# All inputs first, four convolutions in one go, and two expert sums moved to GpSimd, in a kernel of conditional convolution and quantized FFN

## Chip, cores and metric

One core of a Trainium2 chip. The metric is the device time of one execution in microseconds (us), lower is better; the median of repeated runs is compared. Engines: TensorE (PE), VectorE (DVE), ScalarE (ACT), GpSimd (POOL), SyncE (SP). PEld are TensorE's weight loads.

## What is computed

The reference, cut to its core. `x` has 32 tiles of 128 x 2048, `cond` is 32 x 128, there are K = 8 experts of 128 x 128, H = 2048 and I = 1024:

```python
h = gelu(gelu(cond @ W0 + b0) @ W1 + b1)
att = softmax(h @ W2 + b2)                                   # 32 x 8
agg_w = einsum('bk,koi->boi', att, weight)                   # one 128 x 128 matrix per tile
y = einsum('boi,bih->boh', agg_w, x) + (att @ bias_k)[:, :, None]
y = y.astype(bf16)
qg, sg = quant(y * inv_gate); qu, su = quant(y * inv_up)     # per row: max|.|/127, round, clip
gate = (qg @ w_gate.T) * sg * s_wgate
up   = (qu @ w_up.T) * su * s_wup
inter = clip(silu(gate) * up, -10, 10).astype(bf16)
qi, si = quant(inter * inv_inter)
out = x + (qi @ w_down.T) * si * s_wdown
```

## The kernel before

Each of the 32 tiles of x is one unit of work, `t`. For each tile the kernel mixes the eight expert matrices into one (`aggw`), convolves (`conv`, four fp32 matmul calls of 512 columns, each two instructions), writes y as bf16 (`conv_out` on ScalarE), multiplies y by `inv_gate` and reduces each row to its largest value (VectorE: `xg_product`, `xg_scale`, together `quant_g`), forms the codes (ScalarE's `quant_g`), transposes them (on TensorE for the first tiles, by `turn_g`, with an eviction `turned_g` on ScalarE; by a transposing DMA later), and multiplies them with `w_gate` (`gate`, 16 values of `k`, two matmuls each). The up branch is the same with `quant_u`, `turn_u`, `turned_u`, `up`. Then come silu, product, clip, the third quantization and `down`.

Every engine has its instruction order written out by hand, and semaphores join them. Tiles 0 to 3 (`EARLY` = 3, `FIRST` = 4) are handled in a prologue while the weights arrive; from tile 4 on the loop is regular. The change is to the prologue, but for one wait in GpSimd's loop.

Where the expert matrices of the first tiles are mixed:

- tile 0: VectorE sums five experts (`aggregate_first`), TensorE three (`aggregate_mm(0)`), by matmuls with diagonal matrices that ScalarE writes;
- tile 1: ScalarE scales the experts, VectorE reduces them (`experts_sum`, L1082);
- tile 2: GpSimd writes eight diagonal matrices (L465), TensorE sums (`aggregate_mm(2)`, 16 instructions at L538), ScalarE evicts (`aggregate_out`);
- tile 3: the same with VectorE's `diagonals(3)` (L1088);
- from tile 4 on: GpSimd's `aggregate`, four instructions (L442, L444, L446, L450).

`biases_first` (L1041, L1043, L1046) has to be through before `conv_out(0)`. `quant_first` takes tile 0's gate quantization in four chunks of 512 columns (product L1165, reduction L1172). The codes' reciprocal scales are written at L1103; ScalarE's quantization waits for them.

SP's queue loads, in this order: the small MLP inputs, the experts, x0, `inv_gate`, x1, the row vectors, x2, and, once w_gate's first chunk is there, x3. GpSimd's queue issues w_gate's four chunks when x0 has landed, then spreads the row vectors over the partitions (`spread`, L453, six instructions), then w_up's chunks. The weights are fp32 in memory and bf16 in the core's memory.

TensorE's order in the prologue: `conv(0)`, `conv(1)`, `aggregate_mm(2)`, half of `turn_g(0)`, `aggregate_mm(3)`, a quarter of `gate(0)`, the rest of `turn_g(0)`, `conv(2)`, `turn_g(1)`, parts of `gate(0)` and `gate(1)`, `conv(3)`, more of both gates, and so on to `gate(3)`, `turn_u(2)` and `up(0)`. VectorE's: `quant_first`, `diagonals(3)`, `quant_g(1)`, `quant_u(0)`, `quant_g(2)`, `quant_u(1)`, then tile 3.

## Time and profile before

| what | us |
|---|---|
| median of 3 runs | 804.67 (804.56 to 805.69) |
| the profiled execution, its time | 805.92 |
| its span in the profile | 804.1 |
| PE busy | 794.4 |
| DVE busy | 714.6 |
| ACT busy | 441.1 |
| POOL busy | 145.4 |
| DMA engines' mean busy share, first 25 us | 0.91 |

The profile is of one execution. A timeline row gives the start, the duration of the merged instructions, the engine, the source line, the tiles written and read, the count, and in brackets how long the engine stood idle before and what released it. A matmul's duration holds a tail that overlaps the next one. Lines are those of the printed kernel.

### The profile page before, as it was taken

Reading aid. Unit: us, or ns where it says so; the run is one execution under the profiler, and the core shown is the slowest. Engines: PE = TensorE matmul, PEld = TensorE weight load, DVE = VectorE, ACT = ScalarE, POOL = GpSimd, SP = SyncE. Lnnn points to the kernel's source line nnn. Section 1 sums busy time; section 2 is a strip of 40 time slices with the busy share of each in tenths; the row PEclk is TensorE's granted clock in tenths of the full one; section 3 lists DMA queues with packets and bytes.
Section 4 is the critical chain, followed back from the end, with each engine's and each line's share of the span. In section 5 each row is a group of like instructions: output and inputs, shape, how many; then the busy total and the mean of one; then the engine's idle time right before and its main releaser. Section 6 shows DMA issues by size and latency. Waiting matters only on the chain.

```text
span 804.1 us, 9187 instructions
## 1 busy us (share of the span) xinstructions
PE 794.4 (99%) x3521; PEld 365.3 (45%) x3521; DVE 714.6 (89%) x810; ACT 441.1 (55%) x385; POOL 145.4 (18%) x138
## 2 busy tenths in 40 slices
PE   8999999999999999999999999999999999999997
PEld 5454444444444444444444444444444444444443
DVE  6887989999888988888988888988888988888968
ACT  7675235556654546655546655545655546655531
POOL 2603202210222210222210222210222210222000
PEclk9999999999999999999999999999999999999999
DMA  8997745554455444455544355545455544454342
GB/s 296 243 213 148 155 140 171 163 148 141 113 162 160 155 144 117 111 165 157 157 137 125 109 166 156 158 142 101 127 169 154 158 123 143 105 170 151 95 108 105
DMA packets 162964, 119.81 MB, mean 149 GB/s; under 512 B 151780, under 2 KB 152164, under 8 KB 153703
## 3 DMA queue, kind: packets, MB, share of 16 engines
q1 hardware_dynamic: 161192, 106.64, 44.8%
q0 software_dynamic: 1728, 12.58, 7.7%
q8 instruction: 28, 0.46, 0.2%
q14 instruction: 16, 0.13, 0.0%
HBM read 60.48 MB, written 33.55 MB: 117 GB/s over the span
## 4 chain that ended last, share of the span: by engine, by line
PE 90%; DVE 4%; DMA 3%; ACT 1%; issue 1%; SPq 1%; DVEq 0%
PE up_ps L614 26%; PE gate_ps L614 26%; PE down_ps L717 23%; PE conv_ps L567 12%; DMA xt<-x 3%; DVE amax L1093 1%; PE gate_ps L717 1%; ACT qu L853 0%; DMA quT<-qu 0%; DVE down_sc L1257 0%; DVE xt L1266 0%; PE down_ps L572 0%; PE conv_ps L572 0%; DVE region L1111 0%; DVE region L1151 0%
## 5 line engine op out<-in xcount | busy, mean ns | idle before, releaser
L717 PE MATMUL down_ps<-wd,qiT 128*128 128x512 bf16 x896 | 211.2, 379 | 0.0
L614 PE MATMUL gate_ps<-wg,qgT 128*128 128x512 bf16 x928 | 205.7, 379 | 0.0
L614 PE MATMUL up_ps<-wu,quT 128*128 128x512 bf16 x896 | 202.4, 379 | 0.0
L1093 DVE TENSOR_REDUCE amax<-region 128x1 f32<-128x2048 f32 (+1 forms) x90 | 173.0, 1923 | 1.2
L442 POOL TENSOR_TENSOR prod<-wexp,att_bc 128x1024 f32<-128x1024 f32 x28 | 53.1, 1898 | 542.0 <-DVE region L1151 531.0
L717 PEld LDWEIGHTS down_ps<-wd,qiT 128*128 128x128 bf16 x896 | 87.6, 98 | 123.3 <-issue 29.7
L614 PEld LDWEIGHTS gate_ps<-wg,qgT 128*128 128x128 bf16 x928 | 90.7, 98 | 109.5 <-issue 1.1
L614 PEld LDWEIGHTS up_ps<-wu,quT 128*128 128x128 bf16 x896 | 87.7, 98 | 106.1 <-ACT quT L886 0.5
L821 ACT ACTIVATE qg<-region,recip 128x2048 f16<-128x2048 f32 x30 | 60.1, 2002 | 128.1 <-DVE recip L1103 128.1
L567 PE MATMUL conv_ps<-xt,aggw 128*128 128x512 f32 x244 | 117.0, 602 | 2.6 <-DMA xt<-x 1.4
L810 ACT ACTIVATE y<-conv_ps,aggb 128x512 bf16<-128x512 f32 x116 | 78.9, 686 | 60.2 <-PE conv_ps L567 55.6
L1257 DVE SCALAR_TENSOR_TENSOR down_sc<-down_ps,scale,swd_bc 128x512 f32<-128x512 f32 x117 | 86.9, 743 | 0.2 <-PE down_ps L717 0.2
L1266 DVE TENSOR_TENSOR xt<-xt,down_sc 128x512 f32<-128x512 f32 x122 | 84.2, 690 | 3.2
L1204 DVE SCALAR_TENSOR_TENSOR region<-up_ps,scale,swu_bc 128x1024 f32<-128x1024 f32 x28 | 35.9, 1284 | 49.8 <-PE up_ps L614 49.8
L918 ACT ACTIVATE qiT<-qiT 128x1024 bf16<-128x1024 f16 x29 | 30.6, 1056 | 80.8 <-DMA qiT<-qi 80.8
L853 ACT ACTIVATE qu<-region,recip 128x2048 f16<-128x2048 f32 x30 | 60.1, 2004 | 18.1 <-DVE recip L1103 18.1
L567 PEld LDWEIGHTS conv_ps<-xt,aggw 128*128 128x128 f32 x244 | 46.4, 192 | 43.2 <-issue 30.6
L1148 DVE TENSOR_TENSOR region<-y,invg_bc 128x2048 f32<-128x2048 bf16 x27 | 61.7, 2285 | 0.7 <-ACT y L810 0.7
L1151 DVE TENSOR_TENSOR region<-y,invu_bc 128x2048 f32<-128x2048 bf16 x27 | 61.7, 2284 | 0.0
L880 ACT ACTIVATE qgT<-qgT 128x2048 bf16<-128x2048 f16 x27 | 51.6, 1910 | 6.8 <-DMA qgT<-qg 6.8
L888 ACT ACTIVATE quT<-quT 128x2048 bf16<-128x2048 f16 x27 | 51.4, 1902 | 3.2 <-DMA quT<-qu 3.2
L900 ACT ACTIVATE qi<-region,recip 128x1024 f16<-128x1024 f32 x30 | 34.2, 1140 | 15.5 <-DVE recip L1103 15.5
(181 smaller groups left out, 578.9 us busy)
## 6 DMA issues: line engine op xcount, KB each, us to landing
xt<-x SPq DMA_DIRECT2D x30, 1024.0 KB, 4.8
out<-xt SPq DMA_DIRECT2D x29, 1024.0 KB, 4.0
wg<-w_gateT POOLq DMA_DIRECT2D x4, 1024.0 KB, 20.7
wu<-w_upT POOLq DMA_DIRECT2D x4, 1024.0 KB, 17.5
wd<-w_downT POOLq DMA_DIRECT2D x4, 1024.0 KB, 8.2
xt<-x SPq DMA_DIRECT2D x4, 512.0 KB, 4.4
invg_bc<-inv_gate SPq DMA_DIRECT2D x1, 1024.0 KB, 8.5
out<-xt SPq DMA_DIRECT2D x2, 512.0 KB, 2.9
```

The costliest lines, as they stand in the source:

```text
L442: nc.gpsimd.tensor_tensor(prod[:, :, :], wexp[:, :, :], a, ALU.mult).then_inc(pagg_step, 1)
L567: nc.tensor.matmul(conv_bank(t, c), aggw[t % 2][:, :], xcols(t, c), start=True, stop=True).then_inc(conv_done, 1)
L614: last = nc.tensor.matmul(acc[:, n * BANK:(n + 1) * BANK], codes[:, k * P:(k + 1) * P], wts[:, k, n * BANK:(n + 1) * BANK], start=(k == 0) ...
L717: last = nc.tensor.matmul(down_bank(t, c), qiT_at(t)[:, k * P:(k + 1) * P], wd[:, k, c * BANK:(c + 1) * BANK], start=(k == ks[0]), stop=(k ...
L810: nc.scalar.activation(y_at(t)[:, c * BANK:(c + 1) * BANK], conv_bank(t, c), ACT.Identity, scale=norm, bias=aggb[:, t:t + 1]).then_inc(y_r ...
L821: nc.scalar.activation(qg[:, :], xg_at(t), ACT.Copy, scale=trecip(t, 0), bias=ROUND).then_inc(gcodes_ready, 1)
L853: nc.scalar.activation(qu[:, :], xu_at(t), ACT.Copy, scale=trecip(t, 1), bias=ROUND).then_inc(ucodes_ready, 1)
L1093: nc.vector.tensor_reduce(amax[:, i:i + 1], src, axis=AX.X, op=ALU.max, apply_absolute_value=True).then_inc(max_ready, 1)
L1148: nc.vector.tensor_tensor(region1[:, :], y[:, :], invg_bc[:, :], ALU.mult).then_inc(xg_ready, 1)
L1151: nc.vector.tensor_tensor(region2[:, :], y[:, :], invu_bc[:, :], ALU.mult).then_inc(xu_ready, 1)
L1257: nc.vector.scalar_tensor_tensor(down_sc[c % 2], down_bank(t, c), tscale(t, 2), swd_bc[:, c * BANK:(c + 1) * BANK], ALU.mult, ALU.mult).th ...
L1266: nc.vector.tensor_tensor(result_at(t, c), xcols(t, c), down_sc[c % 2], ALU.add).then_inc(result_ready, 1)
```

## The change

- SP's queue loads x2 and x3 right behind x1, ahead of the row vectors; x3 waits for nothing any more. The staging places of the down scales move.
- Tiles 2 and 3: GpSimd multiplies the experts by the attention weights and sums them in three steps (`products`, `sums`) into their own places (`aggw_early`); TensorE's `aggregate_mm(2)` and `(3)`, `diagonals(3)` on VectorE and `aggregate_out` on ScalarE go. The normalization by `erec` moves into `conv_out` of tiles 2 and 3.
- GpSimd's queue: aggregation of tile 2, product of tile 3, two chunks of w_gate when x2 has landed, the sums of tile 3, two more chunks, w_up's first chunk, the spreads, and the rest of w_up.
- TensorE does `conv(0)` to `conv(3)` ahead of any gate work, with `turn_g(0)`'s halves between.
- VectorE and ScalarE do the gate quantizations of all four tiles before any of the up branch.
- y of tile 3, and the scaled y of tile 3, get other places, so that some waits go or are loosened.
- In GpSimd's loop `aggregate(6)` waits for five up products, not six.

```diff
-        Y_HOME = [y[:, :], wd_part(0, bf16), wd_part(1, bf16)]
+        Y_HOME = [y[:, :], wd_part(0, bf16), wd_part(1, bf16), quT[:, :]]
...
-            return Y_HOME[t] if t < EARLY else y[:, :]
+            return Y_HOME[t] if t <= EARLY else y[:, :]
+            if t == EARLY:
+                return XG_HOME[1]
...
-        swd_s = [quT[0:1, :].bitcast(fp32), qu[0:1, :].bitcast(fp32)]
+        swd_s = [wu[:, KH // WCH + 2 * i:KH // WCH + 2 * i + 2, :].rearrange("p k i -> p (k i)").bitcast(fp32)[0:1, :] for i in range(2)]
...
+        aggw_early = {2: qiT[:, 4 * P:6 * P].bitcast(fp32), EARLY: qiT[:, 6 * P:8 * P].bitcast(fp32)}
...
-        diag_at = [region2[:, I:H], prod_flat, region2[:, I:H], prod_flat]
+        diag_at = {0: region2[:, I:H]}
+        weighted = region2[:, I:H].rearrange("p (k r) -> p k r", r=P)
-            i = k - SPLIT if t == 0 else k
+            i = k - SPLIT
...
-            return bank(up_ps, c - 2) if t < EARLY and c >= 2 else bank(conv_ps, c % 2)
+            return bank(up_ps, c - 2) if t <= EARLY and c >= 2 else bank(conv_ps, c % 2)
...
+            sp.dma_start(xslot(2), x[2, :, :]).then_inc(x_in[2], 16)
+            sp.dma_start(xslot(3), x[3, :, :]).then_inc(x_in[3], 16)
-            sp.dma_start(xslot(2), x[2, :, :]).then_inc(x_in[2], 16)
-            sp.wait_ge(wg_in[0], 16)
-            sp.dma_start(xslot(3), x[3, :, :]).then_inc(x_in[3], 16)
...
                                     base=0, pattern=[[-1, P]], channel_multiplier=1).then_inc(ident_set, 1)
-            pool.wait_ge(x_in[0], 16)
-            for i in range(WCH):
-                load(wg, w_gateT, i, wg_in)
+            pool.wait_ge(wexp_in, 16)
             pool.wait_ge(exp_done, 1)
             pool.wait_ge(agg_mm, 1)
-            a = att_bc[:, 2 * K:3 * K].unsqueeze(2).to_broadcast([P, K, P])
-            nc.gpsimd.tensor_tensor(diag_at[2].rearrange("p (k r) -> p k r", r=P),
-                                    ident[:, :].unsqueeze(1).to_broadcast([P, K, P]), a, ALU.mult).then_inc(diag_pool, 1)
+
+            def products(t):
+                a = att_bc[:, t * K:(t + 1) * K].unsqueeze(2).to_broadcast([P, K, P])
+                nc.gpsimd.tensor_tensor(weighted, wexp[:, :, :], a, ALU.mult).then_inc(early_step, 1)
+
+            def sums(t):
+                step = PAGG * (t - 2)
+                pool.wait_ge(early_step, step + 1)
+                nc.gpsimd.tensor_tensor(weighted[:, 0:4, :], weighted[:, 0:4, :], weighted[:, 4:8, :], ALU.add).then_inc(early_step, 1)
+                pool.wait_ge(early_step, step + 2)
+                nc.gpsimd.tensor_tensor(weighted[:, 0:2, :], weighted[:, 0:2, :], weighted[:, 2:4, :], ALU.add).then_inc(early_step, 1)
+                pool.wait_ge(early_step, step + 3)
+                nc.gpsimd.tensor_tensor(aggw_at(t), weighted[:, 0, :], weighted[:, 1, :], ALU.add).then_inc(early_agg, 1)
+
+            products(2)
+            sums(2)
+            pool.wait_ge(early_agg, 1)
+            products(EARLY)
+            pool.wait_ge(x_in[2], 16)
+            for i in range(2):
+                load(wg, w_gateT, i, wg_in)
+            sums(EARLY)
+            for i in range(2, WCH):
+                load(wg, w_gateT, i, wg_in)
+            load(wu, w_upT, 0, wu_in)
             pool.wait_ge(rows_in[0], 16)
...
-            for i in range(WCH - 1):
+            for i in range(1, WCH - 1):
-            pool.wait_ge(wexp_in, 16)
...
-                pool.wait_ge(xu_ready, t)
+                pool.wait_ge(xu_ready, 5 if t == 6 else t)
...
             def aggregate_mm(t):
-                ks = range(SPLIT, K) if t == 0 else range(K)
-                if t == 0:
-                    pe.wait_ge(ident_set, 2)
-                    pe.wait_ge(wexp_in, 16)
-                elif t == 2:
-                    pe.wait_ge(diag_pool, 1)
-                else:
-                    pe.wait_ge(diag_dve, 1)
-                for k in ks:
-                    if t == 0:
-                        pe.wait_ge(diag_act, k - SPLIT + 1)
-                    last = nc.tensor.matmul(agg_ps[t], diag_part(t, k), wexp[:, k, :], start=(k == ks[0]), stop=(k == K - 1))
+                pe.wait_ge(ident_set, 2)
+                pe.wait_ge(wexp_in, 16)
+                for k in range(SPLIT, K):
+                    pe.wait_ge(diag_act, k - SPLIT + 1)
+                    last = nc.tensor.matmul(agg_ps[t], diag_part(t, k), wexp[:, k, :], start=(k == SPLIT), stop=(k == K - 1))
                 last.then_inc(agg_mm, 1)
...
-                        pe.wait_ge(agg_out, t - 1)
+                        pe.wait_ge(early_agg, t - 1)
...
-                    elif t < EARLY or (t == EARLY and c < 2):
+                    elif t <= EARLY:
-                    nc.tensor.matmul(conv_bank(t, c), aggw[t % 2][:, :], xcols(t, c),
+                    nc.tensor.matmul(conv_bank(t, c), aggw_at(t), xcols(t, c),
...
-                        pe.wait_ge(agg_out, 2)
...
-                    if t == 0:
-                        pe.wait_ge(agg_out, 1)
-                    elif t == 1:
-                        pe.wait_ge(y_ready, NC * EARLY)
+                    if t == 1:
+                        pe.wait_ge(y_ready, NC * FIRST)
...
             conv(1)
-            aggregate_mm(2)
+            conv(2)
             turn_g(0, range(1))
-            aggregate_mm(3)
+            conv(EARLY, range(2))
+            turn_g(0, range(1, 2))
+            conv(EARLY, range(2, NC))
             gate(0, range(4))
-            turn_g(0, range(1, 2))
-            conv(2)
-            turn_g(1)
+            turn_g(1, range(1))
             gate(0, range(4, 8))
+            turn_g(1, range(1, 2))
             gate(1, HALVES[0])
-            conv(3)
+            turn_g(2)
             gate(0, range(8, 12))
             gate(1, range(8, 12))
-            turn_g(2)
+            gate(0, range(12, KH))
             turn_u(0)
-            gate(0, range(12, KH))
             gate(1, range(12, KH))
-            gate(2, range(12))
-            turn_g(3)
-            gate(2, range(12, KH))
+            gate(2, HALVES[0])
+            turn_g(EARLY)
+            gate(2, HALVES[1])
             turn_u(1)
-            gate(3)
+            gate(EARLY)
             turn_u(2)
...
-                    elif t == EARLY:
-                        act.wait_ge(xg_ready, 1)
-                        act.wait_ge(xu_ready, 1)
...
-                    norm = erec[:, t:t + 1] if t < 2 else 1.0
+                    norm = erec[:, t:t + 1] if t < FIRST else 1.0
...
-            def aggregate_out(t):
-                act.wait_ge(agg_mm, t)
-                act.wait_ge(conv_done, NC * (t - 1))
-                nc.scalar.activation(aggw[t % 2][:, :], agg_ps[t], ACT.Copy, scale=erec[:, t:t + 1]).then_inc(agg_out, 1)
-
-                if t == 0:
-                    act.wait_ge(row_spread, SWD)
...
+                if t == 0:
+                    act.wait_ge(row_spread, INVI)
+                elif t == 2:
+                    act.wait_ge(xu_ready, FIRST)
...
             quant_g_first(0)
-            aggregate_out(2)
+            conv_out(2, range(2))
+            quant_g_first(1)
+            conv_out(2, range(2, NC))
             turned_g(0, range(1))
-            quant_g_first(1)
-            aggregate_out(3)
+            quant_g(1)
             turned_g(0, range(1, 2))
-            quant_g(1)
-            conv_out(2, range(2))
-            turned_g(1, range(1))
-            conv_out(2, range(2, NC))
-            turned_g(1, range(1, 2))
-            quant_u(0)
-            conv_out(3)
+            conv_out(EARLY)
+            turned_g(1)
             quant_g(2)
             turned_g(2)
+            quant_u(0)
+            quant_g(EARLY)
             turned_u(0)
-            quant_u(1)
-            quant_g(3)
             act.wait_ge(att_dve, Z[1])
             silu(0)
-            turned_g(3)
+            quant_u(1)
+            turned_g(EARLY)
+            turned_u(1)
             quant_u(2)
-            turned_u(1)
             silu(1)
...
-            def diagonals(t):
-                dve.wait_ge(ident_set, 2)
-                dve.wait_ge(agg_sum, 1)
-                a = att_bc[:, t * K:(t + 1) * K].unsqueeze(2).to_broadcast([P, K, P])
-                nc.vector.tensor_tensor(diag_at[t].rearrange("p (k r) -> p k r", r=P),
-                                        ident[:, :].unsqueeze(1).to_broadcast([P, K, P]), a, ALU.mult).then_inc(diag_dve, 1)
-
...
-                    dve.wait_ge(gcodes_ready, 1 if t == 2 else EARLY)
+                    dve.wait_ge(gcodes_ready, t - 1)
...
-                    dve.wait_ge(agg_mm, 2)
+                    dve.wait_ge(early_agg, 2)
-                    dve.wait_ge(gcodes_ready, 2)
+                    dve.wait_ge(gcodes_ready, FIRST)
...
-                    dve.wait_ge(gcodes_ready, EARLY + 1)
+                    dve.wait_ge(gcodes_ready, EARLY)
...
             quant_first()
-            diagonals(3)
             quant_g(1)
+            quant_g(2)
+            quant_g(EARLY)
             quant_u(0)
-            quant_g(2)
+            softmax_rest()
+            gate_out(0)
             quant_u(1)
-            xg_product(3)
-            gate_out(0)
-            xg_scale(3)
-            softmax_rest()
+            gate_out(1)
             xu_product(2)
-            gate_out(1)
             attention_rest()
             gate_out(2)
-            quant_u(3)
-            gate_out(3)
+            quant_u(EARLY)
+            gate_out(EARLY)
             inner_head(0)
             inner_head(1)
```

## Rows read from the trace of the kernel before

**Rows 1.** The page: busy us (share of the span) and instructions of each engine.

```profile
PE 794.4 (99%) x3521; PEld 365.3 (45%) x3521; DVE 714.6 (89%) x810; ACT 441.1 (55%) x385; POOL 145.4 (18%) x138
```

**Rows 2.** Waits of TensorE from 65 us to the end: us, times, longest.

```profile
PE conv_ps L567 <- issue: 0.7, 1, 0.7
PE conv_ps L567 <- ACT y L810: 0.3, 1, 0.3
```

**Rows 3.** Timeline of TensorE in the prologue: start us, us, what, idle before.

```profile
9.40 3.73 PE L567 MATMUL conv_ps<-xt,aggw 128*128 128x512 f32 x4 [0.22 <-DVE aggw L1078]
...
14.69 1.88 PE L567 MATMUL conv_ps<-xt,aggw 128*128 128x512 f32 x4
...
18.12 1.95 PE L538 MATMUL gate_ps<-wexp,region 128*128 128x128 f32 x16
...
26.30 1.98 PE L567 MATMUL conv_ps<-xt,aggw 128*128 128x512 f32 x4 [1.37 <-DMA xt<-x]
...
44.23 1.06 PE L572 MATMUL conv_ps<-ident,qu 128*128 128x128 f16 x16
...
65.08 7.07 PE L614 MATMUL gate_ps<-wu,wd 128*128 128x512 bf16 x32
```

**Rows 4.** Timeline of VectorE in the prologue.

```profile
9.61 0.16 DVE L1046 TENSOR_TENSOR aggb<-aggb,qiT 128x4 f32<-128x4 f32 x1
...
10.05 1.91 DVE L1082 TENSOR_REDUCE aggw<-prod 128x128 f32<-128x1024 f32 x1 [0.28 <-ACT prod L838]
...
12.36 1.45 DVE L1165 TENSOR_TENSOR region<-y,invg_bc 128x512 f32<-128x512 bf16 x1 [0.40 <-ACT y L810]
...
14.44 0.68 DVE L1165 TENSOR_TENSOR region<-y,invg_bc 128x512 f32<-128x512 bf16 x1
...
18.90 0.16 DVE L1103 RECIPROCAL recip<-scale 128x1 f32<-128x1 f32 x1
...
20.12 2.28 DVE L1111 TENSOR_TENSOR wd<-wd,invg_bc 128x2048 f32<-128x2048 bf16 x1
...
24.95 0.16 DVE L1103 RECIPROCAL recip<-scale 128x1 f32<-128x1 f32 x1
```

**Rows 5.** GpSimd: timeline, then its four instructions of one aggregation by windows.

```profile
8.97 2.35 POOL L432 DMA_DIRECT2D wg<-w_gateT  x4 [7.25 <-DMA xt<-x]
...
28.78 1.30 POOL L453 PARTITION_BROADCAST invi_bc<-wd  x1
...
68.30:73.00 4.70, 4.35 (x4) 1.00 0.49 112
```

**Rows 6.** Timelines of GpSimd and VectorE where they meet, near 80 us.

```profile
79.90 1.91 POOL L442 TENSOR_TENSOR prod<-wexp,att_bc 128x1024 f32<-128x1024 f32 x1
...
81.90 2.14 POOL L444 TENSOR_TENSOR prod<-prod 128x512 f32<-128x512 f32 x1
...
80.55 2.36 DVE L1210 TENSOR_TENSOR y<-region,y 128x1024 f32<-128x1024 f32 x1
```

**Rows 7.** Timeline of ScalarE in the prologue.

```profile
11.55 0.78 ACT L810 ACTIVATE y<-conv_ps,aggb,qiT 128x512 bf16<-128x512 f32 x1 [1.29 <-PE conv_ps L567]
...
19.10 1.15 ACT L827 ACTIVATE qg<-region,recip 128x1024 f16<-128x1024 f32 x1
...
24.97 1.02 ACT L860 ACTIVATE qgT<-down_ps 128x1024 bf16<-128x1024 f16 x1 [1.70 <-PE down_ps L572]
...
25.89 2.00 ACT L821 ACTIVATE qg<-wd,recip 128x2048 f16<-128x2048 f32 x1
...
27.78 1.26 ACT L810 ACTIVATE wd<-conv_ps,aggb 128x512 bf16<-128x512 f32 x2
```

**Rows 8.** Landing of x1's and w_up's transfers; queues from 12.5 to 13 us.

```profile
DMA to landing us min/median/max: 11.1/11.1/11.1
...
DMA to landing us min/median/max: 11.3/17.5/24.1
...
q0 software_dynamic: 2, 0.02, 15.6%
```

More of the change, by code:

```diff
@@ L309, in last_half, with aggw_at @@
             return bank(up_ps if h else down_ps, 1 - h)[:, 0:BANK // 2]
+        def aggw_at(t):
+            return aggw_early[t] if t in aggw_early else aggw[t % 2][:, :]
         def xcols(t, c):
```

7 lines of the change are left out of this document (3 added, 4 removed).

## The prediction

> **What bounds the kernel now.** I read the busy shares first: TensorE is busy for 794.4 of 804.1 us [rows 1], so only a few us can come from its waits, and the rest must come from work taken off it. The profiled execution took 805.92 us for its span of 804.1; the three timed runs have a median of 804.67. I make the sum on the span and carry the difference over to the median.
>
> TensorE's waits from 65 us on come to one of 0.7 us and one of 0.3 us [rows 2]. So whatever makes `up(0)` start earlier than its 65.08 us [rows 3] moves the end by the same amount, if all that follows is ordered relative to it. The question of the whole prediction is therefore: when does `up(0)` start in the new order?
>
> **What is removed.** Two of the aggregations on TensorE: 16 fp32 matmuls of 1.95 us for tile 2 [rows 3], and as many for tile 3. Groups overlap by a tail of about 0.16 us (14.69 to 18.12 is 3.43 us for two groups of 1.88), so this is 3.6 us. TensorE also waits 1.37 us for x of tile 2 [rows 3], which now comes before the weights. That is 5.0 us if nothing takes its place: `up(0)` at 60.1. ScalarE loses two small evictions, VectorE loses one product `diagonals(3)`, which stood between 18.9 and 20.1 [rows 4].
>
> **What is added: GpSimd work in the first 22 us.** One aggregation on GpSimd is four instructions, 4.35 us together [rows 5], from 1.9 us for the first down to 0.5 us. Two of them are now done. The first starts when TensorE has finished `aggregate_mm(0)`, which let VectorE go on just before its small biases; I take 9.15 us.
>
> The price is at the port that GpSimd and VectorE share. At 79.90 GpSimd's L442 holds 1.91 us. VectorE's product L1210, which has two operands in SBUF, starts at 80.55 and takes 2.36 us: it ends 1.1 us after GpSimd is through. GpSimd's next instruction at 81.90 has half the elements of L442 and takes 2.14 us: it stood until VectorE's was over [rows 6]. So each holds the other off for a whole instruction. The same is seen at 12.36: VectorE's first product takes 1.45 us, its second 0.68 [rows 4], and GpSimd's L465 follows its four loads, which are through at 11.3 [rows 5]. Reductions (one operand) pass: L1082 at 10.05 takes its normal 1.91 us. Whether tiny two-operand instructions are held too, no row shows, since none met GpSimd at work. It decides much: L1046 (the bias, 0.16 us, at 9.61) and the reduction L1082 behind it stand in the queue ahead of tile 0's quantization. I take them as held, being the same operation with less data; the other end is nothing.
>
> The Trainium skill (GPSIMD Engine Reference, section Specifications) says that GpSimd's SBUF interfaces are "Shared with VectorE (contention with DVE instructions in a 2-port perf mode or with two SBUF inputs)". The rows of large instructions agree; by that rule the tiny ones are held as well, which is the forecast below, and without it the sum is that of the first rival.
>
> **Step 1, when tile 0's scale is ready (r0).** Before, the first product ended at 13.81 and L1103 ended at 19.06 [rows 4]: 5.25 us, of which three more chunks (a product of 0.68 and a reduction) take 1.32 each, and the last reduction with three small instructions 1.3. Now: GpSimd's product of tile 2 holds to 11.25 if VectorE's tiny L1041 gets in just ahead of it (11.05, and one more instruction behind, if not). L1046 follows at 11.4, L1082 runs 11.35 to 13.26, GpSimd's two smaller sums fit beside it to 13.5. First product 13.5 to 14.05. GpSimd's last sum waits for it and ends at 14.5; its product of tile 3 runs 14.6 to 16.5. VectorE's second product, due 14.7, ends at 17.05. GpSimd then issues two weight loads to 18.25, and its next sum lies between the third product (17.7 to 18.35) and the fourth, which ends at 20.2. r0 = 20.2 + 1.3 = 21.5. If GpSimd's product wins the first race, the bias waits for its second instruction as well: the same walk gives 22.7. If tiny instructions pass: 19.8. Before it was 19.06.
>
> **Step 2, when y of all four tiles is ready (Y16).** ScalarE's queue after r0 is, each by its duration less the 0.1 us by which neighbours overlap [rows 7]: half of `quant_g(0)` 1.05, half of `conv_out(2)` 1.36 (two of 0.68: with a scale operand one takes 0.78, against 1.26 for two without), 1.05, 1.36, `turned_g` half 0.92, `quant_g(1)` 1.89, 0.92, and `conv_out(3)` 2.82 to its end. With the start 0.04 that is 11.4 us. TensorE has `conv(2)` done by 21.6 and `conv(3)` within 6 us of r0, so it isn't waited for. Y16 = r0 + 11.4.
>
> **Step 3, when quant_u(0) is ready.** VectorE now does three gate quantizations and only then `quant_u(0)`. One takes 20.12 to 25.11, 4.9 us from one start to the next [rows 4]. Those of tiles 1 and 2 are over about when Y16 comes; tile 3's needs Y16. So R = Y16 + 0.03 + 4.91 + 4.97 = Y16 + 9.9. To this comes a hold by GpSimd's row spreads, 1.30 us each [rows 5]; the last of them falls at about 33 us, where tile 3's product starts: 0 to 1.2 us, I take 0.6. R = r0 + 21.3 + 0.6.
>
> TensorE's own queue arrives sooner: it leaves for `gate(1)` at Y16 + 1.0 (`turned_g(1)`) and has 3.45 + 0.90 + 3 times 1.73 = 9.5 us of work up to `turn_u(0)`, which needs R + 2.1 (2.0 of ScalarE), that is Y16 + 12.0. So VectorE's chain is the later by 1.5 us, and the next thing late is `qu` of tile 0.
>
> **Step 4, from there to up(0).** `turn_u(0)` 0.90, `gate(1)` 1.73, half of `gate(2)` 3.45, `turn_g(3)` 0.90, 3.45, `turn_u(1)` 0.90, `gate(3)` 6.91, `turn_u(2)` 0.90: 19.1 us (44.23 for 16 transposes, 65.08 for 32 matmuls of 7.07, less tails) [rows 3]. Nothing else ends later: after R ScalarE has `quant_u(0)`, `quant_g(3)`, `turned_u(0)`, the exponential with its table load and `silu(0)` (8.6 us), and ends `quant_u(1)` at R + 10.7, wanted at R + 12.4; VectorE has tile 2's scale at R + 15.7, `quant_u(2)` ends at R + 17.7, wanted at R + 20. up(0) = R + 21.2.
>
> Sum: up(0) = r0 + 42.5 + hold. The gain is 65.08 - 42.5 - r0 - hold = 22.5 - r0 - hold. With r0 = 21.5 it is 1.0 less 0 to 1.2; with 22.7 it is -0.2 less the same. Both orders of the race are open; I take +0.3 us: span 803.8, median 804.4.
>
> **What is moved and costs nothing.** x of tile 1 landed 11.1 us after its issue at 3.1, so at 14.2 [rows 8]; at the same pace of 2.5 us a tile x2 lands at 16.8, x3 at 19.3, both before their convolutions at 18.1 and about 23. The row vectors behind them are wanted at 23. The weights pay: their first packets came about 3.6 us after the issue at 8.97 [rows 5, 8]; issued at 17.05 they start at 20.6. A chunk takes 4.9 us, (24.1 - 11.3 + 1.8) / 3 [rows 8], the fourth being issued 1.8 us after the first, so w_gate's chunks land at 25.5, 30.4, 35.3 and 40.2. Wanted, with r0 = 21.5: the first when `turned_g(0)` is through, r0 + 5.9 = 27.4; the second after `quant_g(1)` and a turn, about 30.0; the third and fourth at Y16 + 5.3 and + 8.8, 38.2 and 41.7. The second costs 0.4 us of TensorE, hidden by its wait for Y16. Without that wait it would be paid. w_up's last lands near 60, before 69. `up(0)`'s own first chunk is far ahead.
>
> The earlier `aggregate(6)` takes away the 0.7 us wait ahead of `conv(6)`. But two instructions on, TensorE waits for y, which ScalarE writes after `quant_u(5)` and `silu(4)`; none of these is earlier. The wait of 0.3 us becomes 1.0: worth nothing.
>
> **The rivals.** First, faster: tiny instructions pass GpSimd. r0 = 19.8, gain 2.7 less 0.6: span 802.0, median 802.6. For it: they move almost no data, and the biases might be done before GpSimd is awake. Against: the whole-instruction holds at 12.36 and 80.55. If there were no holds at all r0 would be 18.3 and the gain 4.2 (800.5); the rows speak against it.
>
> Second, slower: TensorE's pace drops. At 9.40 its first four matmuls of the convolution took 3.73 us, where four take 1.88 at 14.69 [rows 3], after a stretch of short gaps; the longest wait after that, 1.37 us at 26.30, dropped nothing. The new order has waits of about 1.0, 1.7 and 1.5 to 2.7 us ahead of `turn_g(0)`, `gate(1)` and `turn_u(0)`. If the last is long enough, the matmuls behind it lose 1.9 us: span 805.7, median 806.3. It decides where a wait goes past what 1.37 us shows to be harmless.
>
> The Trainium skill (TensorE: Matmul & The Clock Gate, Part 1) has the array fall to its lower clock of 1.2 GHz when it has been idle; it gives the mechanism for that rival, and no row here shows a fall after the start.
>
> Third, the whole saving comes through, 5.0 us (799.7): it needs VectorE's chain to `qu` to hide, and that is 5.25 + 4 times 4.9 = 24.9 us of work after its first product, which ended at 13.8: with `quant_u(0)` and the rest of step 4, `up(0)` couldn't start before 60.0 even with no hold and no wait for Y16, which adds 1.6.
>
> **How the numbers follow.** Forecast (saving spent on the holds and on `quant_u(0)` moved behind) 0.52; faster rival, with what lies beyond it, 0.28; pace 0.12; something else late, either side, 0.08. 0.2% is 1.6 us, about what a measurement of this kernel tells from nothing. Faster by more: three quarters of the 0.28, 0.04 of the forecast and 0.03 of the rest, 0.28. Slower by more: most of 0.12, the forecast's worst corner and the rest, 0.17. Within: 0.55. The forecast's own range is 803.6 to 806.1 (hold and race at either end); to hold 8 in 10 it must reach down to the first rival: 802.2 to 806.2.
>
> **What would show it.** Right: L1046 or L1041 stretched to 1 us or more near 9.2 to 11.4; the first product of `quant_first` over by 14 or later; r0 at 21 to 23; ScalarE idle before L827; TensorE waiting at L572 for `qu` near 43 to 45; up(0) at 64 to 66. Wrong: r0 under 20.5; `gate(1)` or `turn_u(0)` waiting for a weight chunk (the queues were misjudged); matmuls of 0.6 us and more behind a wait; a new wait after 65 us.

## The result and the profile after

The changed kernel takes 808.92 us, the median of six runs from 806.79 to 809.44, against 804.99 for the kernel before in the same comparison. The ratio is 1.0041 with a 95% interval of 1.0030 to 1.0051. Slower by 0.4%, where no clear change was forecast and the range ended at 806.2. The profiled execution took 808.85 us:

```profile
span 807.1 us, 9122 instructions
...
PE 793.2 (98%) x3489; PEld 362.3 (45%) x3489; DVE 718.9 (89%) x809; ACT 440.6 (55%) x383; POOL 155.4 (19%) x145
```

TensorE has 1.2 us less work than before [rows 1] (32 matmuls of the expert sums are gone; matmuls that ran slower take part of that back), and the span is 3.0 us longer. Its waits, in the view that names who was waited for (us in total, times, longest):

```profile
PE conv_ps L589 <- ACT qu L857: 2.9, 1, 2.9
...
PE down_ps L589 <- ACT qg L838: 1.9, 1, 1.9
...
PE conv_ps L584 <- ACT y L821: 0.9, 1, 0.9
...
PE up_ps L630 <- ACT wd L864: 0.5, 1, 0.5
```

The wait of 1.4 us for x of tile 2 is gone. In its place stand 1.9 us for tile 0's codes, 0.5 us ahead of `gate(1)` and 2.9 us for `qu` of tile 0. The 0.9 us for y is the one that was 0.3 us [rows 2]. The timeline of TensorE, to be held against [rows 3]:

```profile
17.79 1.88 PE L584 MATMUL conv_ps<-xt,qiT 128*128 128x512 f32 x4
...
23.26 0.62 PE L589 MATMUL down_ps<-ident,qg 128*128 128x128 f16 x8 [1.87 <-ACT qg L838]
...
24.01 3.13 PE L584 MATMUL conv_ps<-xt,qiT 128*128 128x512 f32 x4
...
47.31 1.07 PE L589 MATMUL conv_ps<-ident,qu 128*128 128x128 f16 x16 [2.88 <-ACT qu L857]
...
48.22 3.29 PE L630 MATMUL up_ps<-wg,wd 128*128 128x512 bf16 x8
...
68.12 7.07 PE L630 MATMUL gate_ps<-wu,wd 128*128 128x512 bf16 x32
```

The reader is to see two things. `up(0)` starts at 68.12 us, before it was 65.08: the 3.0 us of the span. And after each long wait the matmuls are slow: four at 24.01 take 3.13 us (1.88 at 17.79), and eight at 48.22 take 3.29 (1.89 is usual). The windows say why; the figure behind the engines' busy times is the granted clock, then the transfer engines' share and GB/s:

```profile
24.00:26.90 2.90, 2.89 (x4) 1.02 (x5) 2.80 (x4) 2.90 (x5) 0.00 (x0) 0.61 0.98 203
...
47.30:51.30 4.00, 3.99 (x24) 1.99 (x25) 3.97 (x3) 3.98 (x5) 0.00 (x0) 0.66 0.95 197
...
60.00:68.00 8.00, 8.00 (x55) 4.23 (x53) 5.61 (x6) 5.78 (x6) 0.42 (x1) 1.00 1.04 213
```

In 24.0 to 26.9 and 47.3 to 51.3 us the mean granted clock is 0.61 and 0.66: for most of the time TensorE is at 1.2 GHz, not at 2.4. It fell behind waits of 1.9 and 2.9 us. It didn't behind the 1.37 us of before [rows 3]. But the length of the wait alone doesn't decide it: runs 1 and 5, which have the same TensorE order, waited at the same place for 1.88 and 2.61 us, and there the clock stayed at 1.00 and the four matmuls took 1.95 and 1.96 us. Run 1 first, then run 5:

```profile
23.47 0.62 PE L589 MATMUL down_ps<-ident,qg 128*128 128x128 f16 x8 [1.88 <-ACT qg L838]
...
24.22 1.95 PE L584 MATMUL conv_ps<-xt,qiT 128*128 128x512 f32 x4
```

```profile
24.46 0.62 PE L589 MATMUL down_ps<-ident,qg 128*128 128x128 f16 x8 [2.61 <-ACT qg L838]
...
25.21 1.96 PE L584 MATMUL conv_ps<-xt,qiT 128*128 128x512 f32 x4
```

The timelines of VectorE and GpSimd are to be held against [rows 4, 5]. VectorE first:

```profile
9.20 1.81 DVE L1046 TENSOR_TENSOR qi<-att_bc,qiT 128x32 f32<-128x32 f32 x1
...
11.27 1.06 DVE L1051 TENSOR_TENSOR aggb<-aggb,qiT 128x4 f32<-128x4 f32 x1
...
14.10 2.07 DVE L1163 TENSOR_TENSOR region<-y,invg_bc 128x512 f32<-128x512 bf16 x1
...
21.86 0.16 DVE L1101 RECIPROCAL recip<-scale 128x1 f32<-128x1 f32 x1
...
33.72 3.32 DVE L1109 TENSOR_TENSOR wd<-quT,invg_bc 128x2048 f32<-128x2048 bf16 x1 [1.77 <-ACT quT L821]
...
39.66 2.86 DVE L1126 TENSOR_TENSOR region<-y,invu_bc 128x2048 f32<-128x2048 bf16 x1
...
45.06 0.16 DVE L1101 RECIPROCAL recip<-scale 128x1 f32<-128x1 f32 x1
```

Of GpSimd, its first product, the last weight issue ahead of the spreads and its first row spread:

```profile
9.07 1.90 POOL L470 TENSOR_TENSOR region<-wexp,att_bc 128x1024 f32<-128x1024 f32 x1 [7.36 <-PE gate_ps L555]
...
22.07 0.55 POOL L437 DMA_DIRECT2D wu<-w_upT  x1
...
32.73 2.30 POOL L458 PARTITION_BROADCAST invu_bc<-wu  x1 [10.11 <-issue]
```

VectorE's two tiny instructions of the biases, 0.18 and 0.16 us alone, take 1.81 and 1.06: each ends as GpSimd's ends. The first product takes 2.07 us, the third 1.27. Tile 0's scale is ready at 22.02 instead of 19.06. The products of tile 3's gate branch and tile 0's up branch take 3.32 and 2.86 us instead of 2.29, both inside the stretch of GpSimd's row spreads. And these begin at 32.73, 10.1 us after GpSimd's issue ahead of them ended at 22.6. The kernel before has such a pause too, 8.79 us:

```profile
22.04 2.54 POOL L453 PARTITION_BROADCAST invu_bc<-wu  x1 [8.79 <-issue]
```

### The profile page after: what moved, and what is told of

Its sections match the earlier page's. It is cut to its first block, busy times and chain, and to the rows that moved or that the text cites. A ratio compares the mean times of both kernels' runs of the same rounds, so it can differ in the third digit from the quotient of the medians.

```text
span 807.1 us, 9122 instructions
## 1 busy us (share of the span) xinstructions
PE 793.2 (98%) x3489; PEld 362.3 (45%) x3489; DVE 718.9 (89%) x809; ACT 440.6 (55%) x383; POOL 155.4 (19%) x145
## 4 chain that ended last, share of the span: by engine, by line
PE 88%; DVE 7%; ACT 2%; issue 1%; DMA 1%; DVEq 0%; ACTq 0%
PE gate_ps L630 26%; PE up_ps L630 26%; PE down_ps L731 23%; PE conv_ps L584 11%; DVE amax L1091 2%; PE gate_ps L731 1%; ACT qu L857 1%; DVE region L1126 1%; DVE region L1163 1%; DMA quT<-qu 0%; DVE wd L1109 0%; PE conv_ps L589 0%; PE down_ps L589 0%; DVE down_sc L1255 0%; DVE xt L1264 0%
## 5 line engine op out<-in xcount | busy, mean ns | idle before, releaser
L1091 DVE TENSOR_REDUCE amax<-region 128x1 f32<-128x2048 f32 (+1 forms) x89 | 170.8, 1919 | 1.2
L832 ACT ACTIVATE qg<-region,recip 128x2048 f16<-128x2048 f32 x29 | 58.1, 2004 | 128.9 <-DVE recip L1101 128.9
L584 PE MATMUL conv_ps<-xt,aggw 128*128 128x512 f32 x232 | 110.3, 598 | 1.6 <-ACT y L821 0.9
L821 ACT ACTIVATE y<-conv_ps,aggb 128x512 bf16<-128x512 f32 x112 | 76.0, 686 | 54.5 <-PE conv_ps L584 50.2
L857 ACT ACTIVATE qu<-region,recip 128x2048 f16<-128x2048 f32 x30 | 60.1, 2002 | 22.5 <-DVE recip L1101 22.5
L584 PEld LDWEIGHTS conv_ps<-xt,aggw 128*128 128x128 f32 x232 | 44.1, 192 | 39.7 <-issue 28.0
L896 ACT ACTIVATE quT<-quT 128x2048 bf16<-128x2048 f16 x27 | 51.3, 1902 | 4.2 <-DMA quT<-qu 4.1
## 6 DMA issues: line engine op xcount, KB each, us to landing
wg<-w_gateT POOLq DMA_DIRECT2D x4, 1024.0 KB, 12.5
```

Source lines behind the costliest of these rows:

```text
L584: nc.tensor.matmul(conv_bank(t, c), aggw_at(t), xcols(t, c), start=True, stop=True).then_inc(conv_done, 1)
L821: nc.scalar.activation(y_at(t)[:, c * BANK:(c + 1) * BANK], conv_bank(t, c), ACT.Identity, scale=norm, bias=aggb[:, t:t + 1]).then_inc(y_r ...
L832: nc.scalar.activation(qg[:, :], xg_at(t), ACT.Copy, scale=trecip(t, 0), bias=ROUND).then_inc(gcodes_ready, 1)
L857: nc.scalar.activation(qu[:, :], xu_at(t), ACT.Copy, scale=trecip(t, 1), bias=ROUND).then_inc(ucodes_ready, 1)
L1091: nc.vector.tensor_reduce(amax[:, i:i + 1], src, axis=AX.X, op=ALU.max, apply_absolute_value=True).then_inc(max_ready, 1)
```

## Experiments

The time of each is given by its ratio to the kernel before, run beside it; the changed kernel has 1.0041. "up(0)" is the start of that product in the profile, 65.08 before and 68.12 after. A gain over the changed kernel is a difference of two such ratios. The intervals of runs 1, 2, 3, 6, 7 and 9 overlap the changed kernel's (1.0030 to 1.0051), so that gains of 1 to 2 us there are likely at best. Each profile shows one execution, and executions differ: the order in which GpSimd and VectorE meet isn't the same in all of them.

**Run 1. The row vectors first.** In the changed kernel's SP queue all row vectors are issued ahead of x2 and x3:

```diff
+            sp.dma_start(rows_s, rows[:, 0:4 * I]).then_inc(rows_in[0], 16)
...
             sp.dma_start(xslot(2), x[2, :, :]).then_inc(x_in[2], 16)
             sp.dma_start(xslot(3), x[3, :, :]).then_inc(x_in[3], 16)
-            sp.dma_start(rows_s, rows[:, 0:4 * I]).then_inc(rows_in[0], 16)
```

> The changed kernel with the row vectors loaded ahead of x of tiles 2 and 3, as the kernel before had them. Theory A (the late rows push GpSimd's spreads onto VectorE's products of tile 3's gate and tile 0's up branch, which took 3.3 and 2.9 us instead of 2.3): the spreads start near 23 us instead of 32.7, both products take under 2.6 us or only one is held, qu of tile 0 is there 1 to 1.6 us sooner, TensorE's wait for it falls from 2.9 to about 1.5 us, and the time falls by 1 to 3 us, by the larger figure if the shorter wait also spares the slow matmuls behind it. Theory B (the spreads are not what matters, GpSimd's sums in the first 22 us are): the time falls by less than 0.6 us.

Ratio 1.0039 (1.0026 to 1.0052). GpSimd's timeline in this kernel, idle time and what ended it in brackets:

```profile
33.27 2.30 POOL L458 PARTITION_BROADCAST invu_bc<-wu  x1 [10.45 <-issue]
```

The spreads start no earlier, at 33.27, and GpSimd stands for 10.45 us before them. So the order of the transfers isn't what holds them, and theory A was wrong in naming late rows. That the spreads hold VectorE's products stays open to this run, since they weren't moved.

**Run 2. Filler in the wait for qu.** 11 matmuls into a PSUM bank that isn't in use:

```diff
+    WARM = 11
...
+            def warm(n):
+                for _ in range(n):
+                    nc.tensor.matmul(conv_ps[:, 0:BANK], wg[:, 0, 0:P], wg[:, 0, 0:BANK], start=True, stop=True)
+
             def turn_u(t):
+                if t == 0:
+                    warm(WARM)
                 pe.wait_ge(ucodes_ready, t + 1)
```

> The changed kernel with 11 matmuls of 512 columns into an unused PSUM bank where TensorE waits for qu of tile 0 (2.4 us of filler in a wait of 2.9 us); they compute nothing that is used. Theory P (the wait lets the pace of the matmuls behind it fall: 8 of them took 3.29 us instead of 1.89): these take 1.9 us again, the granted clock is 1.0 from there on, and the time falls by 1.5 to 2 us, to about 1 us above the kernel before. Rival (the slow matmuls have another cause, such as the weights' transfers): no change, or up to 0.3 us slower.

Ratio 1.0034 (1.0020 to 1.0047). That is 0.6 us better than the changed kernel, which isn't clear of the noise (the medians differ by 1.2 us). Timeline of TensorE in this kernel:

```profile
25.25 3.65 PE L585 MATMUL conv_ps<-xt,qiT 128*128 128x512 f32 x4
...
45.61 2.54 PE L608 MATMUL conv_ps<-wg 128*128 128x512 bf16 x11
...
49.28 1.67 PE L637 MATMUL up_ps<-wg,wd 128*128 128x512 bf16 x7
```

Behind the fillers the product is back to 1.67 us for 7 recorded matmuls, with a granted clock of 1.00, so the idle stretch and the clock are the cause of the slow ones. The convolution at 25.25, where no filler was put, is slow (3.65 us, behind a wait of 3.1). The saving is less than the 1.5 to 2 us expected. In this execution `up(0)` starts at 67.28, only 0.8 us sooner: VectorE's second product met GpSimd's product of tile 3 and took 2.47 us, where it took 0.68 in the profile after, and tile 0's scale came at 23.25.

**Run 3. The biases ahead of GpSimd.**

```diff
             pool.wait_ge(agg_mm, 1)
+            pool.wait_ge(att_dve, BIAS[0])
```

> The changed kernel with GpSimd's first product waiting until VectorE's small biases are through (about 0.9 us later). Theory A (two small VectorE instructions of 0.2 us are held 1.6 and 0.9 us by GpSimd): both take 0.2 us, the reduction behind them starts at 10.1 instead of 12.3, tile 0's scale is ready between 20 and 21.3 instead of 22.0, and up(0) comes 0.7 to 1.8 us sooner. Rival (the holds are only moved to the large products): the scale is ready at 21.7 to 22.5 and the time stays within 0.5 us.

Ratio 1.0020 (1.0004 to 1.0035), some 1.7 us better than the changed kernel. The timelines of VectorE, then of TensorE:

```profile
9.08 0.18 DVE L1047 TENSOR_TENSOR qi<-att_bc,qiT 128x32 f32<-128x32 f32 x1
...
9.52 0.16 DVE L1052 TENSOR_TENSOR aggb<-aggb,qiT 128x4 f32<-128x4 f32 x1
...
21.47 0.16 DVE L1102 RECIPROCAL recip<-scale 128x1 f32<-128x1 f32 x1
```

```profile
31.85 1.90 PE L631 MATMUL gate_ps<-wg,qgT 128*128 128x512 bf16 x8 [1.79 <-DMA wg<-w_gateT]
...
45.38 1.07 PE L590 MATMUL conv_ps<-ident,qu 128*128 128x128 f16 x16 [1.66 <-ACT qu L858]
```

Both tiny instructions take their 0.18 and 0.16 us again. The scale is ready at 21.63, only 0.4 us sooner than in the changed kernel, where theory A had 20 to 21.3 and the rival (the holds only move) 21.7 to 22.5. On this the rival is nearly right: two later products took 2.2 and 1.9 us, because GpSimd's work was moved onto them. `up(0)` nevertheless starts at 64.50, 3.6 us sooner. The wait for `qu` is 1.66 us and no matmul behind it is slow; that the shorter wait is the reason is likely, not shown. The spreads met other instructions: tile 3's product takes 2.29 us, tile 0's 2.72. A new wait shows, 1.8 us for w_gate's second chunk.

**Run 4. GpSimd's sums left out.** GpSimd's product with its three additions is replaced with one addition of two experts, so the weighting of tile 2's and 3's experts is left out:

```diff
             def sums(t):
...
+                nc.gpsimd.tensor_tensor(aggw_at(t), wexp[:, 0, :], wexp[:, 1, :], ALU.add).then_inc(early_agg, 1)
```

> The changed kernel with GpSimd's aggregation of tiles 2 and 3 cut to one small addition of two experts each (the mixing of the experts of those two tiles is left out). Theory A: tile 0's scale is ready at 18.3 to 19 instead of 22.0, all that follows comes 3 to 3.5 us sooner, up(0) starts at 63 to 65 instead of 68.1, and the time falls by 3 to 4 us. Theory W (the weights, issued 7 us later than before, take over as the bound): gate(0) or gate(1) waits for a chunk of w_gate, and the time falls by less than 2 us.

Ratio 0.9995 (0.9979 to 1.0011), 3.7 us better than the changed kernel. VectorE's timeline, then TensorE's:

```profile
12.44 0.69 DVE L1157 TENSOR_TENSOR region<-y,invg_bc 128x512 f32<-128x512 bf16 x1 [0.39 <-ACT y L815]
...
18.23 0.16 DVE L1095 RECIPROCAL recip<-scale 128x1 f32<-128x1 f32 x1
```

```profile
29.71 1.90 PE L624 MATMUL gate_ps<-wg,qgT 128*128 128x512 bf16 x8 [2.13 <-DMA wg<-w_gateT]
```

The first product takes 0.69 us, the scale is ready at 18.39, and `up(0)` starts at 61.27: 6.9 us sooner than in the changed kernel. This is what GpSimd's sums cost there, with what they bring about (no matmul is slow in this run, though TensorE waits 2.1 us, and the weights are issued up to 3 us sooner), and it is more than TensorE's 3.6 us that they replace. But the time doesn't follow in full: this execution's span is 5.5 us shorter than the changed kernel's, the ratio says 3.7. Behind `up(0)` TensorE waits 1.2 us for y and 0.6 for w_down, where the changed kernel waits 0.9. Theory A holds with its 3 to 4 us; of theory W the wait for w_gate's second chunk came, not its bound of less than 2 us.

**Run 5. Another source for the first spread.** It takes its row from x of tile 0 and waits for nothing (`inv_up` is left out):

```diff
+            spread(invu_bc[:, :], xslot(0)[0:1, :])
             pool.wait_ge(rows_in[0], 16)
-            spread(invu_bc[:, :], rows_s[:, 0:2 * I])
```

> The changed kernel whose first row spread takes its row from tile 0's x, which landed at 8.7 us, and waits for no transfer (inv_up is left out, so all that follows from it has other values). Theory L (GpSimd needs about 10 us before its first spread whatever the data, to change to that kind of instruction): the spread still starts about 10 us after GpSimd's last weight issue, near 33 us. Theory R (the row vectors land late): it starts within 1 us of that issue, near 23 us.

There is one execution of it, of 809.02 us, so no ratio is given. GpSimd's timeline:

```profile
33.32 2.30 POOL L458 PARTITION_BROADCAST invu_bc<-xt  x1 [10.83 <-issue]
```

The spread starts 10.8 us after the last weight issue though its data had been there since 9 us. So GpSimd doesn't stand for its data. A pause of the same size, 10.6 to 11.5 us in these kernels, comes where it goes back from spreads to products (before `aggregate(4)`), 11.0 in the kernel before. There the spreads began at 22.0, 8.8 us after the product ahead of them. Run 11, which has no spreads, has no pause before `aggregate(4)`: GpSimd goes from a weight issue to its product at once.

```profile
55.81 1.06 POOL L437 DMA_DIRECT2D wd<-w_downT  x2 [18.92 <-DVE wd L1112]
...
56.88 1.92 POOL L447 TENSOR_TENSOR prod<-wexp,att_bc 128x1024 f32<-128x1024 f32 x1
```

So the pause belongs to the change between products and spreads, in either direction, and weight issues don't bring it.

**Run 6. quant_u(0) ahead of tile 3's gate branch**, on VectorE, and `gate_out(0)` ahead of the rest of the softmax:

```diff
+            quant_u(0)
             quant_g(EARLY)
-            quant_u(0)
+            gate_out(0)
             softmax_rest()
-            gate_out(0)
```

> The changed kernel with VectorE taking the up quantization of tile 0 ahead of the gate quantization of tile 3, and gate_out(0) ahead of the rest of the softmax. Theory A (the order put quant_u(0) last, and TensorE's wait of 2.9 us and the slow matmuls behind it come from that): its scale is ready near 40 us instead of 45.2, TensorE doesn't wait for qu of tile 0, no matmul behind it is slow, up(0) starts at 63.5 to 64.5, and the time falls by 3.5 to 4.5 us, to within 1 us of the kernel before or below it. Rival (the delay moves on to turn_g(3) or gate(2)): up(0) at 66 or later.

Ratio 1.0021 (1.0006 to 1.0035), about 1.6 us better than the changed kernel, where 3.5 to 4.5 was expected. TensorE's timeline:

```profile
45.27 1.06 PE L589 MATMUL conv_ps<-ident,qu 128*128 128x128 f16 x16
```

`turn_u(0)` no longer waits and nothing behind it is slow; `up(0)` starts at 65.51, between what theory A (63.5 to 64.5) and its rival (66 or later) had. `quant_u(0)` can't start before the first spread is done, so VectorE stands for 3.1 us. And in this execution VectorE's second product was held (2.24 us), the scale of tile 0 came at 22.9, with a slow convolution behind it.

**Run 7. The edits of runs 3 and 6 together.**

> As the run before, and GpSimd's first product waits for VectorE's small biases too. Theory A: another 0.5 to 1 us sooner, up(0) at 62.7 to 63.7, faster than the kernel before by 1 to 2.5 us. Theory W (the late weights are the next bound): gate(0) waits 1.8 us or more for w_gate's second chunk, which takes back half or more, and the time is within 0.5 us of the run before.

Ratio 1.0031 (1.0020 to 1.0041), not faster than either. `up(0)` starts at 64.82, where 62.7 to 63.7 was expected, and of TensorE's waits (total us, times, longest) two are

```profile
PE gate_ps L631 <- DVE down_sc L1189: 1.5, 1, 1.5
...
PE down_ps L732 <- DMA wd<-w_downT: 1.1, 1, 1.1
```

The 1.5 us are for `gate_out(0)`, which comes behind two quantizations now, the 1.1 for w_down, and another 1.1 stand ahead of `gate(1)`. The wait for w_gate's second chunk, which theory W had at 1.8 us or more, is 0.5. `up(0)` is 0.3 us ahead of the kernel before, and the span is still 1.6 us longer: in this run time is lost behind `up(0)` as well.

**Run 8. The loosened wait of aggregate(6) alone**, in the kernel before:

```diff
-                pool.wait_ge(xu_ready, t)
+                pool.wait_ge(xu_ready, 5 if t == 6 else t)
```

> The kernel before with only the loosened wait of aggregate(6). The prediction's step: the wait of 0.7 us ahead of conv(6) goes and the wait of 0.3 us for y two groups later becomes 1.0 us, so the time stays within 0.3 us. Rival: 0.7 us faster.

Ratio 0.9997 (0.9983 to 1.0011). TensorE's wait behind the one removed:

```profile
PE conv_ps L567 <- ACT y L810: 0.9, 1, 0.9
```

The wait of 0.7 us is gone and that for y is 0.9 us: worth nothing, as forecast.

**Run 9. Filler in both waits.** As run 2, with 7 more ahead of `turn_g(0)`.

> The changed kernel with filler matmuls in both long waits of TensorE: 7 ahead of the first half of turn_g(0), 11 ahead of turn_u(0); they compute nothing that is used. Theory P (the waits let the matmuls' pace fall, and tile 3's first two convolution calls at 3.1 us for 4 matmuls come from the wait of 1.9 us): these take 1.9 to 2.0 us, no matmul is slow after 14 us, and the median falls to 1.3 to 2.5 us below the changed kernel's, with a spread of the runs of under 1 us. Rival (the first wait's slow matmuls are hidden behind ScalarE): the same as with the one filler, 1 to 1.5 us below.

Ratio 1.0025 (1.0015 to 1.0035), 1.3 us better than the changed kernel (the medians differ by 1.6), its seven runs between 806.88 and 808.31, all with a granted clock of 0.999 or 1.000. TensorE's timeline:

```profile
25.33 1.96 PE L584 MATMUL conv_ps<-xt,qiT 128*128 128x512 f32 x4
...
49.42 1.89 PE L636 MATMUL up_ps<-wg,wd 128*128 128x512 bf16 x7
```

No matmul is slow (1.96 and 1.89 us). `qu` came late in this execution, the slowest of the seven: VectorE's second product was held again, and tile 0's scale came at 23.3.

```profile
16.89 2.52 DVE L1171 TENSOR_TENSOR region<-y,invg_bc 128x512 f32<-128x512 bf16 x1
```

The second filler's own saving can't be told from that of run 2 by the times.

**Run 10. The new order of the loads alone**, in the kernel before, with TensorE's sums kept. GpSimd's product of tile 2 waits for the biases and stands ahead of the four loads of w_gate, which wait for x2:

```diff
             sp.dma_start(xslot(1), x[1, :, :]).then_inc(x_in[1], 16)
+            sp.dma_start(xslot(2), x[2, :, :]).then_inc(x_in[2], 16)
+            sp.dma_start(xslot(3), x[3, :, :]).then_inc(x_in[3], 16)
...
-            pool.wait_ge(x_in[0], 16)
+            pool.wait_ge(att_dve, BIAS[0])
...
+            pool.wait_ge(x_in[2], 16)
...
```

> The kernel before with the new order of the loads alone: x of tiles 2 and 3 right behind x1, w_gate only when x2 has landed, GpSimd's product of tile 2 ahead of them; TensorE keeps its sums and its order. Theory L (whatever GpSimd does after its weight issues waits for them, and its first spread comes some 10 us later): the spreads start near 29 instead of 22 us, quant_u(0)'s product stands from 25 to about 31, gate(0) waits 2 to 3 us for its first chunk, and the time rises by 3 to 7 us. Rival (only the wait of 1.4 us for x2 goes): 0.5 to 1.5 us faster.

Ratio 1.0107 (1.0094 to 1.0120), or 8.6 us, where 3 to 7 was expected. The timelines of GpSimd, VectorE and TensorE, one line of each:

```profile
28.79 2.30 POOL L452 PARTITION_BROADCAST invu_bc<-wu  x1 [10.13 <-issue]
```

```profile
31.12 3.15 DVE L1128 TENSOR_TENSOR region<-y,invu_bc 128x2048 f32<-128x2048 bf16 x1 [6.38 <-POOL invu_bc L452]
```

```profile
43.64 3.78 PE L567 MATMUL conv_ps<-xt,aggw 128*128 128x512 f32 x4 [5.53 <-ACT y L810]
```

The weights are issued at 16.3 to 18.7 us, the first spread starts 10.1 us later, `quant_u(0)`'s product stands for it 6.4 us, and ScalarE and TensorE with it (5.5 us, with slow matmuls behind). No chunk of w_gate was waited for: of theory L that part was wrong. GpSimd's product had ended at 11.9 here, and the pause still comes behind the issues: it begins when GpSimd gets to the spread.

**Run 11. Rows spread by transfers**, and the edits of runs 3 and 6 with it. The other rows go the same way, once w_gate's second chunk is there, and w_up's chunks are issued as those of w_gate land, not behind the spreads:

```diff
-            spread(invu_bc[:, :], rows_s[:, 0:2 * I])
...
+            sp.dma_start(invu_bc[:, :], rows[0, 0:2 * I].partition_broadcast(P)).then_inc(rows_in[0], 16)
```

> The changed kernel with the small biases ahead of GpSimd's first product, quant_u(0) ahead of tile 3's gate quantization, and the row vectors spread by transfers from memory (as inv_gate is) in place of GpSimd's spreads. Theory L+A (spreads come late because GpSimd changes its kind of instruction, and they hold VectorE's products): quant_u(0)'s product starts near 32 instead of 35 us and takes 2.3 us, none of VectorE's products is held after 22 us, turn_u(0) doesn't wait, and up(0) starts at 62.5 to 64. Theory W (3.5 MB more to move, 8 us of the transfer engines, delays weights): gate(0) or up(0) waits for a chunk by 1 us or more and the time is above that of the kernel before.

Its six executions took 815.28 to 830.44 us. The ratio, 1.0188 (1.0137 to 1.0239), is of the two fastest alone (815.28 and 825.64); it is slower, by how much is unclear. The profile is of the execution at 830.44. The timelines of VectorE, then TensorE, then SP's queue:

```profile
31.59 2.29 DVE L1112 TENSOR_TENSOR region<-y,invu_bc 128x2048 f32<-128x2048 bf16 x1
```

```profile
110.54 4.00 PE L717 MATMUL down_ps<-wd,qg 128*128 128x512 bf16 x10 [22.90 <-DMA wd<-w_downT]
```

```profile
68.92 20.16 SPq L374 DMA_TRANSPOSE qgT<-qu  x1
```

In the prologue it went as theory L+A says: the product of `quant_u(0)` takes 2.29 us beside no spreads, `up(0)` starts at 63.36, 1.7 us before that of the kernel before. Then TensorE waits 22.9 us for w_down. The transposing transfer at 68.92 takes 20.2 us to issue, where it takes 1.4 in the kernel before; there the weights issued so far had landed at that time. What makes it so slow was not taken apart, nor whether the executions at 815 us have it, and so no time of this run is put down to the spreads.

**Run 12. x of tile 2 by two queues**, in the kernel before: its second half is issued by ScalarE.

```diff
-            sp.dma_start(xslot(2), x[2, :, :]).then_inc(x_in[2], 16)
+            sp.dma_start(xslot(2)[:, 0:I], x[2, :, 0:I]).then_inc(x_in[2], 16)
...
+            act.dma_start(xslot(2)[:, I:H], x[2, :, I:H]).then_inc(x_part, 16)
```

> The kernel before with the second half of tile 2's x issued by ScalarE, in a transfer queue of its own, at about 10 us. If the queues take turns, x2 lands by 21 instead of 26.2 us, TensorE's wait of 1.4 us for it goes, w_gate's first chunk comes up to 1.5 us later, and the time falls by 0 to 1.3 us. If w_gate's first chunk is then waited for, nothing is gained.

Ratio 1.0031 (1.0019 to 1.0043). TensorE's timeline:

```profile
18.04 3.27 PE L570 MATMUL conv_ps<-xt,aggw 128*128 128x512 f32 x4 [3.59 <-DMA xt<-x]
```

The wait for x2 went, since TensorE got there later, and one of 3.6 us for x1 came. x1 landed 14.9 us after its issue, 11.1 before. The first half of x2 landed at 27.6 us, where x2 had landed at 26.2 and 21 was expected. ScalarE's half, issued at 7.5 us, had landed by 16.6, ahead of x1. But the experts, which landed before ScalarE's issue, came 0.9 us later than before as well, so not all of the delay need be the new queue's; and this execution, 809.39, is the slowest of five (median 807.20). No version tried is clearly faster than the kernel before.

## Why the prediction was wrong, by its own steps

The sum was: up(0) = r0 + 42.5 + hold, with r0 = 21.5 and a hold of 0.6, a gain of 0.4 us. Measured is a loss of 3.0. Two steps failed: step 3, which timed the row spreads by a cause that they don't have and took 0.6 us for a hold of 1.6, and step 4, which had the matmuls behind the wait for `qu` at their usual pace and the clock among the rivals. The difference of 3.4 us is made up so:

| term | forecast | measured | us |
|---|---|---|---|
| r0, tile 0's scale | 21.5 (22.7 in the other order) | 22.02 | 0.5 |
| step 2, r0 to y of all four tiles | 11.4 | 11.65 | 0.25 |
| step 3, hold by the spreads | 0.6 (0 to 1.2) | 1.03 + 0.57 | 1.0 |
| step 4, `turn_u(0)` to `up(0)` | 19.1 | 20.8 | 1.7 |

- **Step 1** came out between its two values, and with some luck. The order that came is the one for which the walk had 22.7: L1046 was held to the end of GpSimd's product and L1051 to the end of its next instruction. The walk also had VectorE's second product held to 17.05. In this execution it passed (0.68 us) and the third took 1.27. In runs 2, 5, 6 and 9 the second was held, for 2.2 to 2.5 us, and the scale came at 22.9 to 23.3. Without GpSimd's sums (run 4) it comes at 18.4; the sum had 18.3.
- **The price at the shared port** was right. Whole-instruction holds, the tiny ones included: shown by the profile after and by run 3, where they vanish. The first rival (they pass) is refuted. The Trainium skill (GPSIMD Engine Reference, section Specifications) names two SBUF inputs as one case of contention, and the trace agrees down to 128x4 elements (1.06 us instead of 0.16). That GpSimd's sums cost more than TensorE's do is shown by run 4, 6.9 us of `up(0)` against 3.6; the 6.9 hold the fall of the clock too.
- **Step 3 failed in its reason and its size.** It had the spreads run from 23 us with the last at 33. They ran from 32.7 to 44.8 and held two products, which take 2.29 us each in run 11, without spreads. The trace of before had the cause in it: GpSimd idle for 8.8 us ahead of its first spread, which I took for the landing of the rows. Runs 1 and 5 show that neither the order of the rows nor their landing matters. The pause comes behind whatever GpSimd did last, product or weight issue, 7.2 to 11.4 us in the kernels here (7.2 in run 12, 8.8 before, 9.5 and more in the others), so it moves with the sums put ahead of it. What GpSimd does in it no run here shows. The Trainium skill (GPSIMD Engine Reference, section 2.1 Instruction dispatch) has the first call to freshly loaded code on GpSimd pay for the loading, about 6 us. No run here shows that this is what happens; the measured pauses are longer, and they come at the change in either direction.
- **Step 4 failed by the clock.** I gave 0.12 to the rival that the clock falls, at 1.9 us; it fell and cost 1.7, the 20.8 in the table against 19.1. The text held 1.37 us of waiting to be harmless and forecast waits of 1.5 to 2.7; the chance was too low for that. The row that the rival's price was taken from, 3.73 us at 9.40, has a granted clock of 1.00 in the profile, so it isn't shown to be a fall of the clock, and that the price came near is luck. Runs 2 and 9 show the cause: with fillers nothing is slow. The first fall cost little: ScalarE waited 0.27 us for the slowed transposes of tile 0, about the 0.25 of step 2. The clock doesn't fall in every execution: of the six of the changed kernel, the one at 806.79 had a granted clock of 1.000 over its span, one at 807.57 had 0.999, and the four at 808.85 to 809.44 had 0.995 to 0.997. So of the median's 3.9 us the clock is worth 1.3 (run 9 by the ratios) to 2.1 (the one execution at 806.79), and 1.8 or more remain without it.
- **The order of VectorE's work** (quant_u(0) last is the next late thing) was right: the wait for `qu` is 2.9 us, and run 6 removes it. That the change of order alone would bring 3.5 us, as expected for run 6, was wrong; the first spread is the next thing.
- **The weights** were rightly found to come when wanted, with the second chunk the tightest: no wait in the changed kernel, 1.8 and 2.1 us in runs 3 and 4, which reach it sooner.
- **That an earlier `up(0)` moves the end by the same amount** held for the changed kernel, 3.0 us for 3.0. It doesn't hold for a gain. `up(0)` starts 0.6, 3.8 and 0.3 us ahead of the kernel before in runs 3, 4 and 7, and the spans are 0.9 longer, 2.5 shorter and 1.6 longer. TensorE's waits behind `up(0)`, 1.0 us before, are 2.0, 1.8 and 2.5 there, with w_down, y and x among them; they explain most of it. So the forecast's gain would have shrunk too.
- **aggregate(6)** was right, by run 8.

Of the 3.4 us by which `up(0)` is later than forecast, then, the clock is 1.7 and its cause shown; the spreads' hold 1.0 and r0 0.5, read from the rows of one execution. Without the fall the kernel is still slower, by 0.2%: the execution at 806.79, and run 9 with 1.0025.

## What to carry to other kernels

Moving work to GpSimd is not free where VectorE is on the path: count for each of its instructions a full stop of whatever two-input VectorE instruction meets it, down to the smallest. An idle stretch in the trace put down to nothing ("issue") is a term of the sum; ask whether it moves with the instruction ahead of it. And where a forecast makes a wait longer than the longest that the trace shows harmless, take the slower clock into the sum and not among the rivals. A pace seen behind one wait doesn't clear the next of the same length.
